# An attention kernel on eight cores: the softmax denominators' reciprocal taken on one row of 1024 instead of by way of two transposes

## What is computed

```python
scores = jnp.einsum('bhqd,bhkd->bhqk', query, key_s) * scaling
attn = jax.nn.softmax(scores, axis=-1)
out = jnp.einsum('bhqk,bhkd->bhqd', attn, v)
...
x = x + _layernorm(attn_ref(_layernorm(x)))
x = x + _layernorm(ffn_ref(_layernorm(x)))
```

## Time and profile before

| | |
|---|---|
| Times of two runs | 4563.4 and 4755.98 us, median 4659.69 |
| Time of the profiled execution | 4551.61 us |
| Its span on the slowest core | 4550.1 us, 42752 instructions (all cores 4518.5 to 4550.1) |
| PE (matmul) busy | 3360.5 us, 74% |
| PEld (weight load) busy | 1339.6 us, 29% |
| ACT busy | 1330.7 us, 29% |
| DVE busy | 899.8 us, 20% |
| POOL busy | 66.6 us, 1% |

### The profile page before, as it was taken

How to read it: one execution, slowest core, us unless ns; L and a number is a source line. 1 busy time by engine, 2 the same in 40 slices (tenths; PEclk the granted TensorE clock), 3 DMA queues, 4 the chain that set the end, 5 groups by cost and what they waited for, 6 DMA issues and landing times. The chain is left out here.

```text
span 4550.1 us, 42752 instructions; the slowest of 8 cores (4518.5 to 4550.1 us)
## 1 busy us (share of the span) xinstructions
PE 3360.5 (74%) x16050; PEld 1339.6 (29%) x16282; DVE 899.8 (20%) x2286; ACT 1330.7 (29%) x1952; POOL 66.6 (1%) x129
## 2 busy tenths in 40 slices
PE   2564964889888898888988889879999048834883
PEld 1332532222222222322222223224444023312331
DVE  3664033110111101111011110100000330023002
ACT  1331101434434344443443434420000330013001
POOL 0000000000000000000000000000000000000000
PEclk9776986989888898898988889879999569976996
DMA  5223301000000000000000000023332326641663
GB/s 149 93 93 61 68 2 31 16 16 16 1 16 16 16 16 1 16 16 16 16 1 16 16 16 1 1 57 73 74 67 45 129 54 110 113 112 38 111 111 111
DMA packets 31369, 218.96 MB, mean 48 GB/s; under 512 B 3888, under 2 KB 4160, under 8 KB 14784
## 3 DMA queue, kind: packets, MB, share of 16 engines
q0 software_dynamic: 17776, 147.97, 17.5%
q1 hardware_dynamic: 13392, 68.24, 4.0%
HBM read 347.37 MB, written 16.78 MB: 80 GB/s over the span
## 5 line engine op out<-in xcount | busy, mean ns | idle before, releaser
L69 ACT ACTIVATE pool<-sPP,pool 128x512 bf16<-128x512 f32 x1024 | 700.1, 687 | 590.0 <-PE sPP L69 589.6
L69 PE MATMUL sPP<-pool 128*128 128x512 bf16 (+1 forms) x1984 | 774.9, 424 | 26.5 <-issue 20.0
L69 PE MATMUL PEp<-pool 128*128 128x512 bf16 (+1 forms) x3839 | 532.3, 290 | 171.5 <-DVE pool L69 92.4
L69 PE MATMUL PDq<-pool 128*1 128x512 bf16 (+3 forms) x1792 | 499.3, 339 | 170.6 <-DVE pool L69 125.5
L69 PE MATMUL fP<-pool 128*128 128x512 bf16 (+1 forms) x2132 | 515.5, 397 | 82.4 <-DMA pool<-wbt 42.0
L69 PE MATMUL oP<-pool 128*128 128x512 bf16 x2007 | 454.4, 387 | 54.0 <-ACT pool L69 31.1
L69 DVE BATCH_NORM_STATS2 pool<-pool 128x6 f32<-128x512 bf16 (+1 forms) x344 | 209.4, 676 | 1285.4 <-ACT pool L69 1211.9
L69 PE MATMUL PCq<-pool 128*128 128x512 bf16 x992 | 419.1, 422 | 0.0
L69 PEld LDWEIGHTS PEp<-pool 128*128 128x128 bf16 (+1 forms) x3872 | 286.2, 97 | 411.1 <-issue 227.0
L69 DVE COPY pool<-PDq 1x1024 f32<-1x1024 f32 x64 | 78.0, 1218 | 1430.9 <-PEq L1242 1396.7
L69 ACT ACT_TABLE_LOAD x77 | 98.8, 1283 | 893.0 <-PE sPP L69 276.7
(11 more groups left out here) (58 smaller groups left out, 1047.6 us busy)
## 6 DMA issues: line engine op xcount, KB each, us to landing
pool<-wbt POOLq DMA_DIRECT2D x64, 1024.0 KB, 8.4
pool<-xb SPq DMA_DIRECT2D x24, 2048.0 KB, 7.6
pool<-wo POOLq DMA_DIRECT2D x16, 2048.0 KB, 13.5
pool<-wqb POOLq DMA_DIRECT2D x16, 1152.0 KB, 8.9
out<-pool SPq DMA_DIRECT2D x64, 256.0 KB, 2.0
pool<-wqa POOLq DMA_DIRECT2D x4, 3072.0 KB, 21.9
pool<-wkvb POOLq DMA_DIRECT2D x16, 512.0 KB, 11.0
pool<-wkva POOLq DMA_DIRECT2D x1, 4608.0 KB, 32.2
```

Source lines behind the costliest of these rows:

```text
L69: r = a(*args, **kw)
```

## The change

The two transposes by TensorE (`kt_tail_t1`, `kt_tail_t2`) and the sections `kt_tail_v2` and `kt_tail_v3` are gone. `kt_tail_v1` now takes the reciprocal of the row `srow_f` itself, 1x1024 in one partition, into the first row of `bcast_sb`, and casts that to `rsum_b`. Both stand ahead of the value projection's copies on VectorE. The broadcast and the multiply are as they were.

```diff
             S_.wait(v, tok[("sums_done", h)])
             v.tensor_copy(out=srow_f[:], in_=PDq[0:1, 0:Q])
-            tok[("srow", h)] = sigV.inc(v.last)
-
-    def kt_tail_t1(blk, h):
...
-            for qb in range(Q // 128):
-                t.transpose(PDq[:, qb:qb + 1],
-                            srow_f[:, qb * 128:(qb + 1) * 128],
-                            ident_f[0:1, 0:1])
...
-    def kt_tail_v2(blk, h):
...
-            v.reciprocal(out=rsumc_f[:], in_=PDq[:, 0:Q // 128])
...
-    def kt_tail_t2(blk, h):
...
-            for qb in range(Q // 128):
-                t.transpose(PDq[0:1, qb * 128:(qb + 1) * 128],
-                            rsumc_f[:, qb:qb + 1], ident_f[:])
...
-    def kt_tail_v3(blk, h):
...
-            v.tensor_copy(out=rsum_b[:], in_=PDq[0:1, 0:Q])
+            t = sigV.inc(v.last)
+            S_.wait(v, t)
+            v.reciprocal(out=bcast_sb[0:1, 0:Q], in_=srow_f[:])
+            t = sigV.inc(v.last)
+            S_.wait(v, t)
+            v.tensor_copy(out=rsum_b[:], in_=bcast_sb[0:1, 0:Q])
             tok[("rsum8_done", h)] = sigV.inc(v.last)
...
             if h + 1 < NH:
                 b_prep_a(blk, h + 1)
-            if h >= 1:
-                kt_tail_t1(blk, h - 1)
-                kt_tail_v2(blk, h - 1)
-            if h + 1 < NH:
                 b_prep_b1(blk, h + 1)
             if h >= 1:
-                kt_tail_t2(blk, h - 1)
-                kt_tail_v3(blk, h - 1)
                 kt_tail_t3(blk, h - 1)
                 kt_tail_v4(blk, h - 1)
```

More of the change, by code:

```diff
@@ L992, in _ @@
             v.tensor_copy(out=srow_f[:], in_=PDq[0:1, 0:Q])
-            tok[("srow", h)] = sigV.inc(v.last)
-    def kt_tail_t1(blk, h):
[L996 to L1000, removed]
-            for qb in range(Q // 128):
-                t.transpose(PDq[:, qb:qb + 1],
-                            srow_f[:, qb * 128:(qb + 1) * 128],
-                            ident_f[0:1, 0:1])
-            tok[("scol_mm", h)] = sigT.inc(t.last)
-    def kt_tail_v2(blk, h):
[L1008 to L1011, removed]
-            v.reciprocal(out=rsumc_f[:], in_=PDq[:, 0:Q // 128])
-            tok[("rsum_done", h)] = sigV.inc(v.last)
-    def kt_tail_t2(blk, h):
[L1016 to L1019, removed]
-            for qb in range(Q // 128):
-                t.transpose(PDq[0:1, qb * 128:(qb + 1) * 128],
-                            rsumc_f[:, qb:qb + 1], ident_f[:])
-            tok[("rsumT_mm", h)] = sigT.inc(t.last)
-    def kt_tail_v3(blk, h):
[L1026 to L1029, removed]
-            v.tensor_copy(out=rsum_b[:], in_=PDq[0:1, 0:Q])
+            t = sigV.inc(v.last)
[4 more added lines that the diff above has]
+            v.tensor_copy(out=rsum_b[:], in_=bcast_sb[0:1, 0:Q])
             tok[("rsum8_done", h)] = sigV.inc(v.last)
@@ L1058, in kt_tail @@
         kt_tail_v1(blk, h)
[L1059 to L1062, removed]
         kt_tail_t3(blk, h)
```

## The result

The changed kernel takes 4519.94 us (median of 11 runs; before 4656.19, median of 10), and the ratio to before is 0.9911, with a 95% interval of 0.9898 to 0.9924. In some executions of any kernel here the cores of one die run at a lower granted clock and the time is some per cent longer; the medians of before lie between such runs and the others (4557 to 4563 us), and the ratios leave them out. The interval leaves out 1, and the change is smaller than the 2% that the prediction took as the least to be told from none. The profiled execution takes 4522.73 us, its span is 4520.9 us. Set against the profiled execution of before, the forecast of 4512 was a ratio of 0.9913; set against the median of 4659.69 beside it, it was 0.968.

The account below looks back on a forecast made before the run. TensorE sets the pace inside a head; at seams, the engine waited for decides. Odd blocks -36.9, even -8.4 and bare seams +5.4 sum to -39.9 us on 4551.61, forecast 4512 us, range 4470 to 4575.

Parts of the forecast that it names:

- the base of the sum: The profiled execution's own 4551.61 us, to which the summed -39.9 us was applied, giving 4512 us (-0.9%).
- The reciprocal: On VectorE, the 1x1024 row was to take 6.6 us, at 6.3 ns a column; upper end 7.8 us.
- Rival A: Reciprocal at eight times the plain copy's pace, 8.6 us; total -5.9 us, 4546 us; chance 0.13.
- rival B: A pipelined reciprocal of 1.2 us; total -75.6 us, 4476 us; chance 0.09.
- t1 gains nothing: Even block: the 0.65 us transposes go, but the value projection still waits for ScalarE until 1633.26; gain nothing.
- Odd blocks: Blocks also projecting queries for two heads: copy out directly behind rope, 2.46 us gained each, 36.9 us over fifteen.
- Even blocks: Blocks with short preparation: value copies 1.65 us late, copy out 0.56 us earlier, 8.4 us gained over fifteen.
- kink: Even blocks: with the reciprocal below some 4.9 us, value copies are not late and the gain stops at 2.2 us.
- Bare seams: Block 31 and the closing block, preparing nothing: 9.95 against 7.24 us, 2.7 us lost each, 5.4 us together.
- Rival C: Even blocks: the new wait before the third value group brings TensorE's clock fall earlier; +75 us, 4587 us; chance 0.08.
- Rival D: Removing a wait leaves four fewer slow main loop units in each of thirty blocks; 103 us, 4409 us; chance 0.04.
- Fit in and delay nobody: Odd blocks: new reciprocal and cast, 7.5 us with gaps, fit into VectorE's 19.7 us wait.

Follow-up runs that it names:

- e2_recip_twice: The changed kernel with the 1x1024 reciprocal done twice; 4652.85 us once, 1.02 of before, the other three times 4814 to 4876 us.
- e3_direct: The changed kernel with one reciprocal reading the sums in PSUM and writing the bf16 row, in place of copy, reciprocal and cast; 0.9901 of before.
- e10_before_rope_early: The kernel before, with only the rope part moved ahead of the value copies on VectorE; 1.0022 of before.
- e12_keep_busy: The changed kernel with useless matmuls in TensorE's idle time at the seams; measured times 4483, 4485, 4546 and 4811 us.
- e14_both_busy: The changed kernel with direct reciprocal, rope early, multiply behind the bias, useless matmuls at seam and loop start; 4238.87 us, 0.93 of before.

## Where the prediction was right, and where it failed

- *The step that failed is the base of the sum.* The -39.9 us were put on the profiled execution (4551.61), while the runs of before that the ratio rests on took 4557 to 4563 us; 40 us off these is about 4520, and 4519.94 was measured. Set against the median of 4659.69 shown beside it, the same 4512 says -3.2%, and measured is -0.9%. The prediction's own reading, -0.9% on a run like the profiled one, came out (0.9913 forecast, 0.9911 measured), but not for its terms alone, as the point on what the sum lacked says.
- *The reciprocal* was to take 6.6 us and takes 6.54. The slope over seven columns held over 1024. Rival A (8.6) is out, and so is rival B (1.2). The Trainium skill ("VectorE: DVE Perf Modes", First, the fixed hardware budget) speaks of a repeat count of eight; measured are (6541 - 164)/1023 = 6.2 ns a column, six times the 1.03 ns of the plain copy, so the measurement decides against eight as a price. The same page of the Trainium skill (Mode 2×_2P) gives a copy of fp32 from SBUF twice the pace of one from PSUM. The trace agrees: the cast takes 681 ns, (681 - 158)/1023 = 0.51 ns a column, with the 158 ns of the one-column copy of rows 9 taken off.
- *t1 gains nothing:* shown, 0.82 us of waiting for ScalarE stand where 0.24 and t1 stood, and the value projection starts no earlier.
- *Odd blocks* were to gain 2.46 us and gained 2.49. e2_recip_twice shows that the reciprocal is free there.
- *Even blocks* were to gain 0.56 and gained 0.90, 13.5 us in all instead of 8.4: the term of the sum that was mis-sized. The place and the mechanism were right (value copies late by 1.5, forecast 1.65; a kink at 2.3, forecast 2.2). Too long were the hand-overs on VectorE: where an instruction doesn't wait for the one ahead of it, it starts 0.07 to 0.08 us before the end of the last one in the timeline (the copy out at 1612.16, the value copy ahead of it until 1612.24), where I had put 0.04 to 0.05 behind it.
- *Bare seams* were to lose 2.7 each and lost 2.73 (the last block), 9.90 us in both.
- *What the sum lacked* is the main loops and the rest of the kernel. Odd loops became 0.68 us shorter and even ones 0.78 longer; that is a loss of only 15 x 0.10 = 1.5 us, by luck, and in e3_direct the same two terms lost 12 us against the changed kernel. Up to the end of attention the mean of the cores gains about 42 us, but only 32.6 in the span: behind attention, which the change doesn't touch, 9 us go lost. This is no scatter of single executions: over the comparable runs (15 of before, 8 of the changed kernel) the mean of the cores' spans falls from 4536.9 to 4505.2 us, by 31.7. The time is that of the slowest core, and it falls by 40 us. So the seams gave 45 us instead of 39.9, loops and the stages behind took some back, and the slowest core gained more than the mean; that this comes to 0.9911 is in part luck. Why the stages behind attention got longer stays open.
- *Rival C* (a fall of the clock within the value projection) doesn't occur at a wait of 1.5 us and does at 4.1 (e10_before_rope_early) and 8.2 (e2_recip_twice). *Rival D* asked for less idle time in the seams. Its prize is real (107 us on the changed kernel), but filling the seam gives only 30 of them; the rest needs the start of the loop, and no part of this change touches that.
- *Missed:* that the order on VectorE before made its idle time useless for what stands behind the small reciprocal. "Fit in and delay nobody" was right for the reciprocal; that nothing on VectorE waits for t1 any longer gives a further 74 us once the rope is moved too, which I had not seen.

## What to carry to other kernels

Idle time of an engine is only free for work that stands ahead of what the engine is waiting for: look at the in-order queue before moving anything into a gap, and value a removed wait by what it lets you move. A long instruction on one partition can be cheaper than two trips through TensorE if it starts early enough, up to the first thing queued behind it. Of changes under 1% read the lengths of the parts, since the same loop, with nothing added to it, took 41.9 to 44.8 us here, for the most part by how many of its units ran at the lower clock.

## What the runs showed of the hardware that I had not expected

- VectorE's reciprocal of a 1x1024 f32 row takes 6541 ns, 6.2 ns a column over the whole length, and as long from PSUM into bf16 (6546 ns). A plain f32 copy of the row takes 691 ns from SBUF and 1212 from PSUM.
- TensorE's granted clock fell in a wait of 1.57 us at the start of the main loop even when the seam ahead of it was filled with matmuls (1.00, then 0.69, then 0.50 in e12_keep_busy), and with that wait filled too it stayed at 1.00 in the loop shown (e14_both_busy).
